# Two cross-attention and feed-forward layers on one core: the first query step of the second attention for four batches at a time, and the output projection started head by head

## The chip, the cores and the metric

The kernel runs on one core of a Trainium2 chip. The metric is the device time of one execution in microseconds (us). Three executions of the kernel before gave 836.81, 837.28 and 837.96 us; the time before is their median, 837.28 us.

## The reference, cut to what matters

The input `x` has B = 8 batches of T = 100 tokens and D = 512 features, and every batch has a context of 361 rows of 128 numbers. Each of two layers adds an attention over the context and a feed-forward part to `x`. The change touches only the second attention and what follows it:

```
q_hk   = layernorm(x) @ Wq.T                      # 16 heads of 128
q_r    = (q_hk @ w_kc_q) @ W_qr                   # 64 numbers per head
k_r    = rope(ctx) @ W_kr                         # per head
attn   = softmax(q_r . k_r)                       # 100 x 361 per head
ctx_c  = attn @ rope(ctx)                         # 128 numbers per head
x     += (ctx_c @ w_kc_kv.T, all heads) @ Wo.T
x     += ffn of the second layer, weights and activations rounded to 8 bits
```

## The kernel before, in words

Nearly all products are made in three parts: an operand is split into a rounded high part (made by ScalarE, ACT) and a low part (made by VectorE, DVE), and `mm3` (lines 149 to 151) runs high x high, high x low and low x high. Each engine has its own program, and semaphores tie them together.

**Preparation.** The query weights are folded into `NFH`/`NFL` (line 1333 and around): eight blocks of 128 columns, each with two heads of 64. `ln_transposes`, `ln_high`, `ln_low` and `normalise` (lines 107 to 131) bring the normalised tokens of a batch into `XHC`/`XLC`. They use two PSUM banks in turn.

**Queries.** `pe_queries` makes the queries of two batches (a pair q = 0..3) in 12 steps. Steps 0 to 3 are the first step: each makes two head blocks, 4 chunks x 3 parts x 2 blocks = 24 products of 200 columns (two batches of 100 tokens), and ACT and DVE (`act_queries` line 949, `dve_queries` line 1791) move 400 columns out into `QRH`/`QRL`. Steps 4 to 11 are the second step: products of 64 rows with `WKH`/`WKL` (line 1363), two heads at a time, moved out into `QH`/`QL` by the same two lines. The first pair's queries come before the attention; those of pair q are made during the second batch of the pair before.

**Attention.** A batch has 1600 rows (16 heads x 100 tokens), that is 13 tiles of 128. Per tile: scores S (mm3 of 362 columns), maximum on DVE (`nmx`, line 1810), exponential on ACT (line 973), normalisation on POOL (line 831), transposes PT on PE (line 1407), high and low part (`pt_hi` line 979, `pt_lo` line 1813), and, per group of tiles, the products PV with the values (384 or 448 columns), which ACT moves out (`ctxo`, line 987). `pair_steps` is a table of ticks: 13 S ticks of the first batch, 13 of the second, then 12 query ticks PR. Everything else is placed behind its due tick; the last five PT of a pair fall on query ticks 0, 2, 4, 6 and 8. All engines walk through this one table: batch 0, then a loop of three passes over (odd batch, even batch), then batch 7 ("last").

**Output.** `pe_fold_p` (line 1384) folds the output weights of the 16 heads; ACT makes `pf_hi` (line 1123) and DVE `pf_lo` (line 1993). The context rows come back from memory in 7 tiles of 128 tokens (`load_ctx`, line 714), are split by `split_ctx` (line 1119) and `low_ctx` (line 1989), and `project(n, ...)` makes 16 heads x 3 products of 512 columns into bank 6, which `add_out` (line 2003) adds to the tokens. Then the last feed-forward part runs, its first products in line 1589; projections 2 to 6 lie between its products in quarters.

SP issues the loads in the order of its program. The folded weights' loads (`load_foldp`), the first context tile, the feed-forward weights `W1Q`, `S1B`, `W2Q`, `S2B` and the later context tiles follow each other there.

Of the kernel before, what the change touches and what calls it, by code (L numbers as in the profile page):

```python
# [96 lines left out]
def build_kernel(nc, x, ctx_t, wq0_t, wkv0_t, wout0_t, ident_d, mask_d, wg_t, w12_d, w3_d, route_d,  # L97
                 ctxn_d, cos_d, sin_d, foldq_d, krt_d, foldp_d,
                 wup_d, wdown_d, wupt_d, wdownt_d, out):
    with ExitStack() as top:  # L100
# [171 lines left out]
        YG_PLACES = [YG_AT + 4 * D * i for i in range(9)] + [2 * FQB + 4 * D * i for i in range(4)] + [W3_AT + 4 * D * i for i in range(3)]  # L272
# [13 lines left out]
        QRH = sc_("qr_hi", [128, NP1, 2 * T], F32R)  # L286
        QRL = sc_("qr_lo", [128, NP1, 2 * T], F32R)
# [18 lines left out]
        FPR_PLACES = [25600, 41984, 47104, 52224, 58368, 65536, 73728]  # L306
# [59 lines left out]
        FPR.append(wraw[:, 0:2 * FP].rearrange("p (h n) -> p h n", h=2))  # L366
# [162 lines left out]
        def _(sp):  # L529
# [155 lines left out]
            for b in range(B):  # L685
# [10 lines left out]
                for g in range(NG):  # L696
# [8 lines left out]
                    elif b == B - 1 and g < 3:  # L705
# [9 lines left out]

            load_foldp(NP1 - 1)
# [4 lines left out]
            sp.dma_start(W2Q[:, :, :], w2_scratch).then_inc(FFNW, 16)  # L721
            sp.dma_start(S2B[:, :], sc_scratch[0:1, 2 * FI:2 * FI + D].broadcast_to((128, D))).then_inc(FFNW, 16)
            for n in range(1, NTT):
                load_ctx(n)
                if n == 2:
# [12 lines left out]
        def _(pool):  # L738
# [48 lines left out]
            pool.wait_ge(E["ups"], NBLK)  # L787
# [12 lines left out]
            def rope(n, j, part):  # L800
# [22 lines left out]
            def pool_steps(kind, n, j):  # L823
                for step in attention_steps(kind):
# [21 lines left out]
            with pool.Fori(0, B // 2 - 1) as p:  # L846
                pool_steps("odd", 2 * p + 1, 1)
# [89 lines left out]
        def queries_part(k, hi):  # L937

            if k < 4:
                o = (QRH if hi else QRL)[:, 2 * k:2 * k + 2, :]  # L940
# [1267 lines left out]
```

## Time and profile before

| | |
|---|---|
| median of three executions | 837.28 us |
| the profiled execution's own time | 830.72 us |
| its span in the trace | 828.9 us |
| granted TensorE clock, mean of the span | 0.932 |
| PE busy | 690.5 us (83%) |
| DVE busy | 510.2 us (62%) |
| ACT busy | 416.0 us (50%) |
| POOL busy | 247.3 us (30%) |
| share of PE in the chain that ended last | 59% |

The profiled execution is one execution with its own time; its span is the part between the first and the last recorded instruction. PE is TensorE's matmuls, PEld its weight loads, which overlap with the matmuls. The granted clock is a share of full speed: 0.5 is the lower level of 1.2 GHz, 1.0 the upper one of 2.4 GHz. The stages are: first attention until 165 us, routing and experts until 354 us, folding and gathering until 394 us, second attention until 645 us, output projection and last feed-forward part until 829 us.

### The profile page before, as it was taken

To read this page: it belongs to the slowest core of one execution; us is meant where nothing else is said; L and a number is where in the kernel's file an instruction comes from. 1 tells how busy PE (TensorE), PEld (TensorE's weight loads), DVE (VectorE), ACT (ScalarE), POOL (GpSimd) and SP (SyncE) were. 2 spreads that over 40 slices of the span, in tenths; PEclk is the share of its full clock that TensorE was granted. 3 is DMA by queue.
4 is the path that set the end of the run, shared out by engine and by line. 5 is a ranking of instruction groups with operands and counts; after the bars stand their busy time and mean duration, and the time that the engine had idled before them with its cause. 6 is when DMAs were issued, how large, how long until landed. Compare 5 with 4: busy or idle time off the path is not lost.

```text
span 828.9 us, 13011 instructions
## 1 busy us (share of the span) xinstructions
PE 690.5 (83%) x4427; PEld 552.5 (67%) x4427; DVE 510.2 (62%) x1038; ACT 416.0 (50%) x777; POOL 247.3 (30%) x278
## 2 busy tenths in 40 slices
PE   0799999654999999992988988988988698799985
PEld 0587777453777777692867877878867375566542
DVE  4876677474666666538476476476475623677674
ACT  3513566363555555321377477476475522455452
POOL 2000742332122222054066166085073001122232
PEclk9987999765999999996799999999999999999997
DMA  8565842598675665698001223123257952111000
GB/s 260 192 209 145 297 147 59 185 390 302 188 228 176 188 184 162 206 297 202 12 1 50 60 50 85 42 60 77 64 172 201 387 191 70 52 52 39 13 14 28
DMA packets 82964, 118.90 MB, mean 143 GB/s; under 512 B 40769, under 2 KB 63037, under 8 KB 79329
## 3 DMA queue, kind: packets, MB, share of 16 engines
q1 hardware_dynamic: 79777, 109.71, 41.6%
q0 software_dynamic: 3136, 8.53, 4.1%
q8 instruction: 30, 0.49, 0.2%
q14 instruction: 21, 0.17, 0.1%
HBM read 97.15 MB, written 27.62 MB: 151 GB/s over the span
## 4 chain that ended last, share of the span: by engine, by line
PE 59%; DVE 15%; ACT 9%; issue 8%; DMA 5%; POOL 1%; ACTq 1%; SPq 0%; DVEq 0%; POOLq 0%
PE PS L149 14%; PE PS L151 12%; PE PS L150 12%; PE PS L1231 4%; PE PS L1407 3%; PE PS L1292 3%; PE PS L1589 2%; DMA raw<-wkv_in 2%; DMA yg<-ys_scratch,slots 2%; DVE nmx L1810 2%; ACT w_hi L884 1%; PE PS L1384 1%; ACT cx_hi L1119 1%; DMA cx_raw<-tile_scratch 1%; ACT wraw L973 1%
## 5 line engine op out<-in xcount | busy, mean ns | idle before, releaser
L831 POOL TENSOR_TENSOR wraw<-wraw,rinv 128x361 f32<-128x361 f32 (+1 forms) x104 | 80.9, 787 | 127.2 <-DVE rinv L1803 126.3
L1646 DVE TENSOR_TENSOR w_lo<-w,w_hi 128x1408 fp32r<-128x1408 f32 x40 | 64.9, 1623 | 39.7 <-ACT w_hi L884 39.7
L973 ACT ACTIVATE wraw<-PS,nmx 128x361 f32<-128x361 f32 (+1 forms) x104 | 58.6, 564 | 30.8 <-DVE nmx L1810 17.8
L1810 DVE TENSOR_REDUCE nmx<-PS 128x1 f32<-128x361 f32 (+1 forms) x104 | 55.1, 531 | 30.3 <-PE PS L151 30.3
L859 POOL TENSOR_TENSOR wraw<-gs,us 128x352 f32<-128x352 f32 (+1 forms) x28 | 26.7, 953 | 139.8 <-ACT gs L1147 112.2
L1813 DVE TENSOR_TENSOR pt_lo<-PS,pt_hi 128x384 fp32r<-128x384 f32 (+1 forms) x104 | 55.7, 535 | 16.3 <-ACT pt_hi L979 15.0
L884 ACT CAST w_hi<-w 128x1408 fp32r x40 | 54.7, 1369 | 18.6 <-DMA w<-w_in 9.4
L784 POOL DMA_INDIRECT xb<-xn_scratch,rows x20 | 31.8, 1589 | 106.6 <-PE PS L1203 103.5
L1407 PE MATMUL PS<-ident,wraw 128*128 128x128 f32 x312 | 52.2, 276 | 11.3 <-DVE pt_lo L1813 5.5
L149 PE MATMUL PS<-w_hi,xt_hi 128*128 128x352 f32 x160 | 56.9, 355 | 5.6 <-DVE xt_lo L1640 5.4
L149 PE MATMUL PS<-pf_hi,cx_hi 128*128 128x512 f32 (+1 forms) x112 | 48.1, 429 | 11.8 <-DVE x_tiles L2003 4.5
L1231 PE MATMUL PS<-w,ht 128*128 128x512 f32 (+1 forms) x120 | 54.9, 593 | 0.7 <-DVE ht L1658 0.7
L979 ACT CAST pt_hi<-PS 128x384 fp32r<-128x384 f32 (+1 forms) x104 | 48.4, 466 | 11.9 <-PE PS L1407 11.8
L1407 PEld LDWEIGHTS PS<-ident,wraw 128*128 128x128 f32 x312 | 38.1, 140 | 23.1 <-issue 10.9
L151 PE MATMUL PS<-w_hi,xt_lo 128*128 128x352 f32 x160 | 52.5, 328 | 0.0
L150 PE MATMUL PS<-w_lo,xt_hi 128*128 128x352 f32 x160 | 52.4, 328 | 0.0
L151 PE MATMUL PS<-pf_hi,cx_lo 128*128 128x512 f32 (+1 forms) x112 | 45.6, 407 | 0.0
L150 PE MATMUL PS<-pf_lo,cx_hi 128*128 128x512 f32 (+1 forms) x112 | 45.5, 406 | 0.0
L149 PE MATMUL PS<-kt_hi,q_hi 128*128 128x362 f32 (+1 forms) x104 | 42.2, 405 | 2.0 <-DVE q_lo L1791 2.0
L149 PE MATMUL PS<-pt_hi,kn_hi 128*128 128x384 f32 (+1 forms) x96 | 36.2, 377 | 9.0 <-ACT ctxo L987 3.8
L115 PE MATMUL PS<-ident,xn 100*128 100x100 f32 x64 | 10.8, 312 | 38.9 <-DVE xn L129 38.1
L149 PEld LDWEIGHTS PS<-w_hi,xt_hi 128*128 128x128 f32 x160 | 30.9, 193 | 18.3 <-DVE xt_lo L1640 18.3
(270 smaller groups left out, 1937.1 us busy)
## 6 DMA issues: line engine op xcount, KB each, us to landing
w<-w_in SPq DMA_DIRECT2D x20, 768.0 KB, 5.5
w<-w_in SPq DMA_DIRECT2D x8, 1408.0 KB, 11.4
fq_raw<-foldq_in SPq DMA_DIRECT2D x6, 1088.0 KB, 7.8
cx_raw<-tile_scratch SPq DMA_DIRECT2D x6, 1024.0 KB, 5.1
ys_scratch<-yb SPq DMA_DIRECT2D x20, 256.0 KB, 5.5
ctx_scratch<-ctxo SPq DMA_DIRECT2D x24, 192.0 KB, 1.9
fp_raw<-foldp_in SPq DMA_DIRECT2D x7, 640.0 KB, 5.0
wraw<-wup_in SPq DMA_DIRECT2D x12, 256.0 KB, 4.3
```

The lines of the kernel that those rows point to most:

```text
L149: pe.matmul(o, lh, rh, start=start, stop=False)
L150: pe.matmul(o, lh, rl, start=False, stop=False)
L151: return pe.matmul(o, ll, rh, start=False, stop=stop)
L831: pool.tensor_tensor(P1[slot][0:rows, 0:NK], P1[slot][0:rows, 0:NK], rinv[0:rows, jj, t:t + 1].broadcast_to((rows, NK)), ALU.mult).then_in ...
L884: act.copy(WH[which][:, :], w12_of(act_whi.e, which)).then_inc(WHS[which], 1)
L973: act.activation(P1[t % 8][r, 0:NK], PS[r, t % 4, 0:NK], ACT.Exp, bias=nmx[r, jj, t:t + 1], accum_out=rsum[r, jj, t:t + 1]).then_inc(C["ex ...
L979: act.copy(pt_place(PTH, t), turned(t)).then_inc(C["pth"], 1)
L1231: last = pe.matmul(PS[:, 4 + i % 2, :], HT[i % 2][0:rows, c * 128:(c + 1) * 128], W3R[i % 2][0:rows, c * D:(c + 1) * D], start=(c == 0), s ...
L1407: last = pe.transpose(PS[:, 4 + t % 3, c * 128:(c + 1) * 128], P1[t % 8][:, c * 128:(c + 1) * 128], ident[:, :])
L1646: dve.tensor_tensor(WL[which][:, :], w12_of(dve_wlo.e, which), WH[which][:, :].bitcast(F32), ALU.subtract) \
L1810: dve.tensor_reduce(nmx[r, jj, t:t + 1], PS[r, t % 4, 0:NK], AX.X, ALU.max, negate=True).then_inc(C["max"], 1)
L1813: dve.tensor_tensor(pt_place(PTL, t), turned(t), pt_place(PTH, t).bitcast(F32), ALU.subtract) \
```

## The change

1. The first query step is done for four batches at once: 8 steps, one head block each, 12 products of 400 columns. It is run for pairs 0 and 2 alone (16 query ticks); pairs 1 and 3 have only the 8 ticks of the second step, which reads its half of the 400 columns. `QRH` and `QRL` are twice as large. Before the attention, four batches are normalised and turned instead of two.
2. The loops of the second attention are written out on all engines.
3. Output: projection 0 no longer waits for all 16 low parts of the folded weights but for one head at a time; projection 1 goes to bank 7 and doesn't wait for `add_out(0)`; projection 2 waits for `add_out(0)` alone. Context tile 0 is split after head 9 instead of head 12, tile 2 before `act_xev(0, 0)`. `W2Q` and `S2B` are loaded behind context tile 1 instead of ahead of it.
4. Places in SBUF move: the gathered expert rows, and folded weights 6, which are now loaded when all transposes of the last batch are done.

```diff
-        def pair_steps(last, vector):
+        def pair_steps(last, vector, asked):
             ticks = [("S", b, t) for b in range(2) for t in range(RT)]
-            ticks += [("PR", 2, k) for k in range(12)] if not last else []
+            ticks += [("PR", 2, k) for k in asked] if not last else []
...
+        FIRST, SECOND = 8, 8
+        def asked_in(q):
+            return range(FIRST + SECOND) if q % 2 == 0 else range(FIRST, FIRST + SECOND)
+        def asked_at(q, k):
+            return 24 * (q // 2) + (k if k < FIRST else k + q % 2 * SECOND)
...
-                if i == NP1 - 1:
+                if i >= NP1 - 2:
                     sp.wait_ge(C["pt"], RT * B)
...
+            load_foldp(NP1 - 2)
             load_foldp(NP1 - 1)
             load_ctx(0)
...
-            sp.dma_start(W2Q[:, :, :], w2_scratch).then_inc(FFNW, 16)
-            sp.dma_start(S2B[:, :], ...).then_inc(FFNW, 16)
             for n in range(1, NTT):
                 load_ctx(n)
+                if n == 1:
+                    sp.dma_start(W2Q[:, :, :], w2_scratch).then_inc(FFNW, 16)
+                    sp.dma_start(S2B[:, :], ...).then_inc(FFNW, 16)
...
-            if k < 4:
-                for m in (2 * k, 2 * k + 1):
-                    for c in range(KC):
...
-                        last = mm3(pe, PS[:, k, m % 2 * 2 * T:(m % 2 + 1) * 2 * T], NFH[:, c, m * 128:(m + 1) * 128],
-                                   NFL[:, c, m * 128:(m + 1) * 128], xh, xl, c == 0, c == KC - 1)
+            if k < FIRST:
+                bank_free(k)
+                x = slice(q // 2 * 4 * T, (q // 2 + 1) * 4 * T)
+                for c in range(KC):
+                    last = mm3(pe, PS[:, k % 4, 0:4 * T], NFH[:, c, k * 128:(k + 1) * 128], NFL[:, c, k * 128:(k + 1) * 128],
+                               XHC[:, c, x], XLC[:, c, x], c == 0, c == KC - 1)
...
-            with pe.Fori(0, B // 2 - 1) as p:
+            for p in range(B // 2 - 1):
                 pe_steps(pe, "odd", 2 * p + 1, 1, p + 1)
                 pe_steps(pe, "even", 2 * p + 2, 0)
...
-                if h == NH0 - 4:
+                if h == NH0 - 7:
                     split_ctx(0, 0)
...
-                    wait(pe, O["res"], n)
+                    wait(pe, O["res"], n if n > 2 else n - 1)
                 for h in heads:
+                    if n == 0:
+                        pe.wait_ge(O["pfl"], h + 1)
...
-            pe.wait_ge(O["pfl"], NH0)
...
+                if n == 0:
+                    pe.wait_ge(O["res"], 2)
...
-            ln_low(dve, 2, 0, XHC, XLC)
-            normalise(dve, 2, 2)
-            ln_low(dve, 2, 1, XHC, XLC)
-            normalise(dve, 2, 3)
+            for b in range(B // 2):
+                ln_low(dve, 2, b, XHC, XLC)
+                normalise(dve, 2, b + 2)
```

The first place is DVE's queue between the last maximum of an odd batch (`nmx` 64x1, not shown) and the first maximum of the next batch, in the query ticks. `qr_lo` is the first step's low part, `q_lo` the second step's, `pt_lo` that of a transposed tile. Before, in every pass:

```order
L1791 TENSOR_TENSOR qr_lo<-PS,qr_hi 128x400
L1813 TENSOR_TENSOR pt_lo<-PS,pt_hi 128x3x128
...
L1791 TENSOR_TENSOR q_lo<-PS,q_hi 128x2x2x100
L1813 TENSOR_TENSOR pt_lo<-PS,pt_hi 128x3x64
...
L1791 TENSOR_TENSOR q_lo<-PS,q_hi 128x2x2x100
L1810 TENSOR_REDUCE nmx<-PS 128x1
```

Now, for the queries of pairs 1 and 3:

```order
L1813 TENSOR_TENSOR q_lo<-PS,q_hi 128x2x2x100
L1835 TENSOR_TENSOR pt_lo<-PS,pt_hi 128x3x128
...
L1813 TENSOR_TENSOR q_lo<-PS,q_hi 128x2x2x100
L1835 TENSOR_TENSOR pt_lo<-PS,pt_hi 128x3x64
L1832 TENSOR_REDUCE nmx<-PS 128x1 x2
```

For pairs 1 and 3 the four `qr_lo` are gone, the five last `pt_lo` lie between the eight `q_lo`, and the 64-column `pt_lo` comes behind the last of them. For pair 2 eight `qr_lo` come first, all but one of the last five `pt_lo` lie between them, and seven `q_lo` follow with nothing between.

The second place is ACT's queue behind the second attention: `pf_hi` are the folded weights' high parts, `cx_hi` the context tiles', `xqt` the turned feed-forward input. Before:

```order
L1123 CAST pf_hi<-PS 128x512 x13
L1119 CAST cx_hi<-cx_raw 128x2048
L1123 CAST pf_hi<-PS 128x512 x3
L1119 CAST cx_hi<-cx_raw 128x2048
...
L1134 ACTIVATE xn_end<-xn_end,mgc,wraw 128x512
L1141 COPY xqt<-PS 128x512
L1119 CAST cx_hi<-cx_raw 128x2048
```

Now:

```order
L1141 CAST pf_hi<-PS 128x512 x10
L1137 CAST cx_hi<-cx_raw 128x2048
L1141 CAST pf_hi<-PS 128x512 x6
L1137 CAST cx_hi<-cx_raw 128x2048
...
L1152 ACTIVATE xn_end<-xn_end,mgc,wraw 128x512
L1137 CAST cx_hi<-cx_raw 128x2048
L1159 COPY xqt<-PS 128x512
```

Tile 0's split moved three heads ahead, and tile 2's ahead of the copy that lets the feed-forward part start. DVE's `cx_lo` of tile 0 moved in the same way, from behind 14 heads to behind 11.

## Rows read from the trace of the kernel before

**Rows 1.** Busy time by stretch, one loop pass: us, then each engine's busy time, clock, DMA
```profile
504.00:563.00 59.00, 53.35 (x378) 47.26 (x378) 35.55 (x93) 36.98 (x103) 28.01 (x37) 1.00 0.27 62
```
**Rows 2.** Timeline of PE, queries of a pair: start us, us, engine, line; 18 products apart
```profile
520.19 0.27 PE L149 MATMUL PS<-xnTc_hi,nf_hi 128*128 x1
...
522.20 0.28 PE L149 MATMUL PS<-xnTc_hi,nf_hi 128*128 x1
```
**Rows 3.** Timeline of PE, first attention, products of 400 columns, 36 apart
```profile
57.77 0.34 PE L149 MATMUL PS<-xnT_hi,hi 128*128 128x400 f32 x1
...
64.36 0.34 PE L149 MATMUL PS<-xnT_hi,hi 128*128 128x400 f32 x1
```
**Rows 4.** Timeline of PE, queries of pair 0, 18 products apart, and batch 0's first score
```profile
398.64 0.41 PE L150 MATMUL PS<-xnTc_lo,nf_hi 128*128 128x200 f32 x1
...
402.48 0.41 PE L150 MATMUL PS<-xnTc_lo,nf_hi 128*128 128x200 f32 x1
...
419.72 0.43 PE L149 MATMUL PS<-kt_hi,q_hi 128*128 128x362 f32 x1 [1.97 <-DVE q_lo L1791]
```
**Rows 5.** Busy time by stretch: query ticks 0 to 3, then 4 to 11, of pair 2
```profile
516.20:529.90 13.70, 13.70 (x115) 13.37 (x114) 3.46 (x7) 3.82 (x8) 0.90 (x2) 1.00 0.24 54
529.90:538.18 8.28, 7.48 (x71) 6.25 (x71) 5.99 (x12) 5.11 (x13) 0.00 (x0) 1.00 0.20 49
```
**Rows 6.** Groups of DVE's instructions, 395 to 646 us: busy us, mean ns, idle before
```profile
L1813 DVE TENSOR_TENSOR pt_lo<-PS,pt_hi 128x384 fp32r<-128x384 f32 (+1 forms) x104 | 55.7, 535 | 16.3 <-ACT pt_hi L979 15.0
...
L1791 DVE TENSOR_TENSOR q_lo<-PS,q_hi 128x400 fp32r<-128x400 f32 x32 | 17.4, 569 | 3.1 <-ACT q_hi L949 3.0
```
**Rows 7.** Timeline of PE's weight loads: first of a pass; first behind the loop
```profile
494.60 0.19 PEld L149 LDWEIGHTS PS<-kt_hi,q_hi 128*128 128x128 f32 x1 [0.26 <-issue]
...
612.19 0.19 PEld L149 LDWEIGHTS PS<-kt_hi,q_hi 128*128 128x128 f32 x1
```
**Rows 8.** Timeline of DVE and PE, batches normalised ahead of the queries
```profile
397.08 0.57 DVE L125 TENSOR_TENSOR xnTc_lo<-PS,xnTc_hi 128x400 fp32r<-128x400 f32 x1
397.56 0.54 DVE L129 TENSOR_SCALAR xn<-X,mv,rstd 100x512 f32<-100x512 f32 x1
...
398.33 0.52 PE L149 MATMUL PS<-xnTc_hi,nf_hi 128*128 128x200 f32 x1
```
**Rows 9.** Timeline from the folded weights to the first feed-forward products, with idle and releaser
```profile
646.46 8.82 PE L1384 MATMUL PS<-fp_raw 128*128 128x512 f32 x20 [1.93 <-DVE pf_lo L1993]
...
657.97 2.28 DVE L1989 TENSOR_TENSOR cx_lo<-cx_raw,cx_hi 128x2048 fp32r<-128x2048 f32 x1
...
661.51 0.50 PE L149 MATMUL PS<-pf_hi,cx_hi 128*128 128x512 f32 x1 [4.51 <-DVE pf_lo L1993]
...
662.66 0.63 PE L150 MATMUL PS<-pf_lo,cx_hi 128*128 128x512 f32 x1
663.09 0.63 PE L151 MATMUL PS<-pf_hi,cx_lo 128*128 128x512 f32 x1
...
675.45 0.47 PE L149 MATMUL PS<-pf_hi,cx_hi 128*128 128x512 f32 x1 [1.15 <-DVE x_tiles L2003]
...
686.45 0.40 PE L1578 MATMUL PS<-identb,xq 128*128 128x128 bf16 x4
...
687.62 1.35 PE L1589 MATMUL PS<-w1q,xqt 128*128 128x352 bf16 x8 [0.77 <-ACT xqt L1141]
...
692.34 0.47 PE L149 MATMUL PS<-pf_hi,cx_hi 128*128 128x512 f32 x1 [3.37 <-DVE x_tiles L2003]
...
696.76 1.37 PE L1589 MATMUL PS<-w1q,xqt 128*128 128x352 bf16 x8
```
**Rows 10.** DMA issues, 600 to 720 us (KB, us to landing), and the split of tile 1
```profile
s_rows<-sc_scratch SPq DMA_DIRECT2D x1, 1408.0 KB, 16.9
w2q<-w_scratch SPq DMA_DIRECT2D x1, 1408.0 KB, 19.4
...
670.47 1.91 ACT L1119 CAST cx_hi<-cx_raw 128x2048 fp32r<-128x2048 f32 x1 [12.16 <-DMA cx_raw<-tile_scratch]
```

More of the change, by code:

```diff
@@ L471, in group_cols, with projected_bank @@
             return ROWS - 384 * g if g == NG - 1 else 384
+        def projected_bank(n):
+            return 7 if n == 1 else 6
         def tile_rows(t):
@@ L821, in rope_low, with pool_steps @@
                 pool.tensor_tensor(KNL[j][:, :, :], kvr[:, :, :], KNH[j][:, :, :].bitcast(F32), ALU.subtract).then_inc(C["knl"], 1)
-            def pool_steps(kind, n, j):
-                for step in attention_steps(kind):
+            def pool_steps(kind, n, j, q=None):
+                for step in attention_steps(kind, q):
                     what, dn, t = step
@@ L966, in act_steps @@
         def act_steps(act, kind, n, j, q=None):
-            for what, dn, t in attention_steps(kind):
+            for what, dn, t in attention_steps(kind, q):
                 m, jj = (n, j) if dn == 0 else (n + dn, 1 - j)
@@ L1102, in _ @@
             lnc_act(act)
-            ln_high(act, 2, 0, XHC)
-            ln_high(act, 2, 1, XHC)
+            for b in range(B // 2):
+                ln_high(act, 2, b, XHC)
             act_keys(act, 0, 0)
-            for k in range(12):
-                if k % 2 == 0:
-                    ln_high(act, 2, 2 + k // 2, XHC)
+            for k in asked_in(0):
+                if k < FIRST and k % 2 == 0:
+                    ln_high(act, 2, B // 2 + k // 2, XHC)
                 act_queries(act, 0, k)
             act_steps(act, "even", 0, 0)
-            with act.Fori(0, B // 2 - 1) as p:
+            for p in range(B // 2 - 1):
                 act_steps(act, "odd", 2 * p + 1, 1, p + 1)
@@ L1362, in pe_queries @@
                             r = slice(half * R1, (half + 1) * R1)
-                            last = pe.matmul(PS[:, (k + half) % 4, (m - k + 4) * 2 * T:(m - k + 5) * 2 * T], w[r, m, :], x[r, m, :],
+                            last = pe.matmul(PS[:, (k + half) % 4, (m - heads[0]) * 2 * T:(m - heads[0] + 1) * 2 * T], w[r, m, :], x[r, m, mine],
                                              start=(x is QRH and w is WKH), stop=(w is WKL), tile_position=(half * R1, 0))
@@ L1387, in pe_steps @@
         def pe_steps(pe, kind, n, j, q=None):
-            for what, dn, t in attention_steps(kind):
+            for what, dn, t in attention_steps(kind, q):
                 m, jj = (n, j) if dn == 0 else (n + dn, 1 - j)
@@ L1803, in invert @@
                 dve.reciprocal(rinv[r, jj, t:t + 1], rsum[r, jj, t:t + 1]).then_inc(C["inv"], 1)
-            for what, dn, t in attention_steps(kind, vector=True):
+            for what, dn, t in attention_steps(kind, q, vector=True):
                 m, jj = (n, j) if dn == 0 else (n + dn, 1 - j)
@@ L1981, in _ @@
             dve_steps(dve, "even", 0, 0)
-            with dve.Fori(0, B // 2 - 1) as p:
+            for p in range(B // 2 - 1):
                 dve_steps(dve, "odd", 2 * p + 1, 1, p + 1)
```

95 lines of the change are left out of this document (49 added, 46 removed).

## The prediction

> **What bounds the kernel now.** I read the time by stretch first, then PE's timeline in the stretches that the change touches, then the idle times there, DVE's groups, and last the DMA issues.
>
> In one pass of the second attention's loop (59 us for two batches) PE is busy 53.35 us, DVE 35.6, ACT 37.0, at the full clock [rows 1]. So PE is the bound. In the query ticks this is stronger: in ticks 0 to 3, the first query step, PE is busy for all of 13.70 us and DVE for 3.5; in ticks 4 to 11, the second step, PE is busy 7.48 of 8.28 us and DVE 5.99 [rows 5]. The first is pure PE time, the second is close to a chain PE, ACT, DVE. Behind the attention, PE waits 4.51 us before projection 0, 1.15 us before projection 1 and 3.37 us before projection 2 [rows 9]. These waits are on DVE, on the path that ends last.
>
> **The price of a product.** 18 products of 200 columns start 2.01 us apart: 0.112 us each [rows 2]. 36 products of 400 columns, also with a new weight load each, take 6.59 us: 0.183 us [rows 3]. Two of the first cost 0.223 us, one of the second 0.183. Per four batches, 192 products become 96. The first step of pairs 0 and 1 (or 2 and 3) costs 192 x 0.112 = 21.4 us before and 96 x 0.183 = 17.6 now: 3.8 less, twice, 7.6 in all if the clock is full and nothing else comes to bind.
>
> The Trainium skill speaks against this term: "TensorE: Matmul & The Clock Gate", Back-to-back issue gap, gives the isolated gap at the upper clock as columns / 2.4 + 2.5 ns. As an estimate by that page, two products of 200 columns take 171.7 ns and one of 400 takes 169.2, so the term would be 0.5 us, not 7.6. Rows 2 disagree with it for the small product (112 ns against 85.8); the page itself says that weight loads count in a real stream.
>
> **Part by part, in the second attention.**
>
> Pair 0 gets longer. (a) Two more batches are turned first. On DVE each costs 0.57 us for the low part and 0.54 for normalising [rows 8]: 2 x 1.11, with the last turn's latency about +2.5 us; queries start near 400.8 instead of 398.33. (b) The clock is at its lower level here: 0.213 us per product [rows 4], until about 402.9, just behind these rows. Before, 22 products at 0.213 and 74 at 0.112 made 13.0 us. At the lower level a product of 512 columns takes 0.43 us [rows 9], so one of 400 takes 0.43 x 400 / 512 = 0.34. If the clock rises at the same moment, 6 products at 0.34 and 90 at 0.183 make 18.5 us: +5.5. (c) All four remaining turns now lie inside the first step, two more than before, some 0.4 us each: +0.8. (d) The second step loses them: its eight `q_lo` at 0.569 [rows 6] and a lead of about 1 us make 5.5 us, where before it took 419.72 - 398.33 - 13.0 - 0.8 (two turns) = 7.6 [rows 4, 8], with four low parts and three normalisings between: -2.1. Sum **+6.7 us**. Bounds: +6.0 if the turns overlap better, +8.5 if the clock rises one or two microseconds later (each costs 0.45).
>
> Pairs 1 and 3 lose 96 x 0.112 = 10.7 us each. Their cover goes too: the last five transposed tiles, two of which lay under ticks 0 to 3, now share eight ticks with the eight `q_lo`. DVE then has 8 x 0.569 + 5 x 0.535 = 7.2 us [rows 6] in about 11 us, and its last `pt_lo` stands behind the last `q_lo`, with PV and the next scores behind it. The second step already shows 0.8 us of idle PE in 8.28 [rows 5]; I double the stalls' density over the longer piece: +1.7 us. So **-9.0 us each**, between -10.7 (no stall) and -6 (ACT and DVE bind all through, 1.1 us a tick more than PE needs).
>
> Pair 2 grows by 96 x (0.183 - 0.112) = +6.8 us. Its second step has no transposed tiles left, save one, and becomes a chain bound by DVE of 5.5 us; the PE work moved out of it now lies in the PE-bound first half. Idle PE grows from 0.8 to perhaps 1.6: **+7.6 us**, between 6.5 and 8.5.
>
> Writing out the loops: a pass begins with a PE wait of 0.26 us for issue that the batch behind the loop doesn't have [rows 7]. Three passes, less what the wait hides: **-0.5 us**, bounds -0.8 and 0.
>
> By the Trainium skill, "Runtime: NRT & Kernel Launch", Instruction fetch mechanics, a taken branch to code outside the two resident blocks costs a fetch by DMA. Rows 7 show 0.26 us at the jump, so I take this value; a fetch at each jump would add gains that no row here shows.
>
> Attention in all: 6.7 - 18.0 + 7.6 - 0.5 = **-4.2 us**.
>
> **Part by part, behind the attention.**
>
> Projection 0 now starts where the first head's low part and `cx_lo` are there. PE makes ten heads in 8.82 us, 0.88 each [rows 9]. ACT's split (1.91 us as for tile 1 [rows 10]) comes three heads earlier, but the context tile is then just landing; DVE's 2.28 us for `cx_lo` then stand ahead of `pf_lo` of head 11, for which PE's head 15 waits. The fold is delayed by about 3 us and ends near 660.2 instead of 661.51 - 4.51 = 657.0; projection 0 follows at once, near 660.2 instead of 661.51: **-1.3 us**, between -2.5 and +0.5.
>
> PE's longest idle time falls from 4.51 us to about 2. Before, the clock fell behind it: products of 512 columns took 0.43 us [rows 9]. Projection 0 took 13.94 - 1.15 = 12.8 us, projection 1 the same 48 products in 11.0. The idle time of 1.93 us ahead of the fold was not followed by such a fall, so I take the full clock: **-1.7 us**, or 0.
>
> Projection 1 waited 1.15 us for `add_out(0)`. Bank 7 removes that. Its other need, context tile 1, landed only at 670.47 [rows 10], because W2Q and S2B were ahead of it in the queue; W2Q landed 2.5 us (plus 0.5 between the issues) behind S1B [rows 10]. Without both, tile 1 lands some 4 us earlier, near 666.5, its high and low parts (1.9 and 2.3 us) are done at 670.7, and projection 0 ends at 671.2. So the wait goes whole: **-1.2 us**, or +1 if the tile lands no earlier.
>
> Between projection 1's end at 686.45 and projection 2's start at 692.34 lie 5.9 us: turn, 0.77 us of waiting, 1.35 of gate and up, and 3.37 of waiting for split, `cx_lo` and `add_out(1)` of the old order [rows 9]. Tile 2 is now split ahead of `xqt`, and `add_out(1)` is not waited for. 2.5 us remain: **-3.4 us**, or -1 if tile 2, which waits for W2Q and S2B now, lands late. The quarter of projection 2 then took 696.76 - 692.34 = 4.4 us for 12 products, against 12 x 0.229 = 2.75 at the full clock: **-1.6 us**, or 0 if the clock falls here all the same.
>
> The rest of the feed-forward part hangs on this start through PE, DVE and the tile loads, and I let it move as a whole. Sum -9.2 us. The loads of folded weights 6 come 3 us later, behind the last transposes; head 12 needs them 7 us after that, so nothing. The memset of POOL that waits for the last expert products ends before the stores it waits for anyway: nothing.
>
> **Sum.** -4.2 - 9.2 = -13.4 us. Against the profiled execution's own 830.72 us that is 817.3. The median, 837.28, is 6.6 us above that one; I subtract the same amount there: **823.9 us**.
>
> **Rivals.**
>
> *A, half the tail.* The clock falls behind the shorter idle times too and the rest of the feed-forward part gives back part of the start, since it waits for DVE in places. The loss is 1.7 + 1.6 + about 1.5: 828.7. For it: PE still rests about 2 us between single heads before projection 0. Against it: 1.93 us did no harm.
>
> *B, the short ticks bind.* In pairs 1 and 3 ACT and DVE set the pace: -6 instead of -9, twice: 829.9. For it: DVE's 7.2 us and ACT's equal load in 11 us, in chains. Against it: the second step runs with PE 90% busy now.
>
> *C, columns are all that counts.* The 400-column product costs twice the 200-column one, 0.223 us: the 7.6 us are gone, 831.5. Rows 3 are the same kind of product at 0.183, so little speaks for it.
>
> *D, slower, by the written-out code.* Two further copies of the loop's body are fetched. A pass has 378 products and 378 weight loads on PE [rows 1], so some 1500 more instructions in blocks that could stall PE at each fetch. It decides from 13.4 us on over, say, six blocks, 2.2 us each; at 5 us each it would be 853. Against it: batch 7 stands outside the loop, and its first score is issued without even the 0.26 us [rows 7].
>
> *E, no change.* The clock stays low through pair 0's whole first step: 90 x (0.34 - 0.183) = +14 us, 838. The chip would have to keep it low under a busy PE, while before it rose after 8 us.
>
> **How the numbers follow.** A measurement of this kernel can tell about 0.2%, 1.7 us, from no change. Chances: forecast 0.58 (820 to 827), A 0.17, B 0.10, C 0.06, E 0.03, D 0.04, and 0.02 for more than the forecast. Forecast, A, B, and C lie over 1.7 us below: with the last, 0.93 faster. E is 0.03 same. D is 0.04 slower. The range 819.5 to 831 takes in the forecast's unknowns (all lower bounds -9, upper +5), A and B.
>
> **What would show it.** In the profile after: first-step products 0.18 us apart, 96 per four batches; pair 0's first score near 426.5; from the first score of batch 2 to that of batch 4, and of 4 to 6, 66.5 and 50 us instead of 59 twice (pair 2's queries lie in the first, pair 3's in the second, pair 1's ahead of both); projection 0 at the full clock, projection 1 with no wait, projection 2 within 3 us of projection 1's end. Wrong it would be if PE stands idle over 3 us in the queries of pairs 1 and 3, if a stretch of written-out code shows waits for issue, or if the last part of the kernel, from projection 2 on, takes longer than now.

## The result and the profile after

The changed kernel took 826.0 us (median of four executions, 824.61 to 829.34), the kernel before 837.62 beside it on the same chip (836.81 to 838.48): a ratio of 0.9863, 95% interval 0.982 to 0.9906, or 11.6 us less. The forecast was 823.9, range 819.5 to 831.

The traces don't show 11.6 us. The profiled execution of the changed kernel took 826.05 us, just its median; the one of before had been 830.72, 6 us under the fastest execution timed beside it. Against that profiled execution the prediction had 817.3 us, and 826.05 is 8.7 more. So the two are compared stretch by stretch. The changed kernel's page (first line, part 1, and the first line of part 4):

```profile
span 824.0 us, 12030 instructions
...
PE 688.8 (84%) x4235; PEld 550.3 (67%) x4235; DVE 511.2 (62%) x1038; ACT 416.0 (50%) x777; POOL 249.4 (30%) x278
...
PE 55%; DVE 14%; issue 13%; ACT 8%; DMA 4%; POOL 2%; ACTq 1%; SPq 1%; another core or an unknown queue 0%; DVEq 0%; POOLq 0%
```

PE is as busy as before (690.5 us there): fewer products, but more of them at the low clock. Its timeline in the queries of pair 0 (start us, us, engine, line; in brackets the idle time before and what ended it), beside [rows 4]:

```profile
402.87 0.68 PE L149 MATMUL PS<-xnTc_hi,nf_hi 128*128 128x400 f32 x1
403.36 0.54 PE L150 MATMUL PS<-xnTc_lo,nf_hi 128*128 128x400 f32 x1
...
407.69 0.38 PE L151 MATMUL PS<-xnTc_hi,nf_lo 128*128 128x400 f32 x1
407.91 0.35 PE L149 MATMUL PS<-xnTc_hi,nf_hi 128*128 128x400 f32 x1
...
423.92 0.36 PE L1381 MATMUL PS<-qr_hi,wkr_hi 64*128 64x200 f32 x2
...
430.71 0.67 PE L149 MATMUL PS<-kt_hi,q_hi 128*128 128x362 f32 x1 [1.61 <-DVE q_lo L1813]
```

Its busy times over the first two parts of that (us, then each engine's busy time, clock, DMA):

```profile
402.87:407.69 4.82, 4.82 (x17) 4.77 (x15) 1.25 (x3) 0.92 (x2) 0.81 (x1) 0.50 0.00 0
408.00:423.90 15.90, 15.90 (x94) 15.52 (x92) 5.71 (x11) 4.14 (x9) 0.00 (x0) 1.00 0.00 1
```

The first 15 products run at the low clock, 0.333 us apart; the rest are 0.183 apart. Behind the attention, beside [rows 9] and [rows 10] (timeline of PE, ACT and DVE):

```profile
655.07 1.90 ACT L1137 CAST cx_hi<-cx_raw 128x2048 fp32r<-128x2048 f32 x1 [1.20 <-DMA cx_raw<-tile_scratch]
...
658.10 2.28 DVE L2010 TENSOR_TENSOR cx_lo<-cx_raw,cx_hi 128x2048 fp32r<-128x2048 f32 x1
658.33 1.10 PE L1402 MATMUL PS<-wraw 128*128 128x512 f32 x2 [1.64 <-DVE pf_lo L2014]
...
661.04 2.07 PE L1402 MATMUL PS<-wraw 128*128 128x512 f32 x2 [1.61 <-DVE pf_lo L2014]
662.12 1.42 PE L149 MATMUL PS<-pf_hi,cx_hi 128*128 128x512 f32 x1
663.33 0.63 PE L150 MATMUL PS<-pf_lo,cx_hi 128*128 128x512 f32 x1
663.76 0.63 PE L151 MATMUL PS<-pf_hi,cx_lo 128*128 128x512 f32 x1
...
669.09 1.91 ACT L1137 CAST cx_hi<-cx_raw 128x2048 fp32r<-128x2048 f32 x1 [5.35 <-DMA cx_raw<-tile_scratch]
...
686.73 0.40 PE L1598 MATMUL PS<-identb,xq 128*128 128x128 bf16 x4
687.89 1.35 PE L1609 MATMUL PS<-w1q,xqt 128*128 128x352 bf16 x8 [0.77 <-ACT xqt L1159]
688.96 0.52 PE L149 MATMUL PS<-pf_hi,cx_hi 128*128 128x512 f32 x1
691.85 1.37 PE L1609 MATMUL PS<-w1q,xqt 128*128 128x352 bf16 x8
```

Projection 2 starts 2.2 us behind the turn of xq instead of 5.9, without a wait, and its first quarter is over after 2.9 us instead of 4.4. But PE waits twice in the fold (1.64 and 1.61 us), and projection 0 still starts at the low clock (0.43 us a product).

The same stretches in all the traces, worked out from starts in PE's timeline, in us. "q0", "q1" ... are the queries of pair 0, 1 ...: q0 from the first turn to the first score of batch 0, the others from the last score of the batch ahead to the first of the next; "to last" from the first turn to the last score; "P0" from there to projection 0; "P0-xq" on to the first turn of xq; "xq-P2" on to projection 2; "quarter" on to its second quarter. From there to the end it is 129.5 to 132.3 us in all of them. A score is the product of keys and queries (`kt_hi,q_hi`), a turn the transpose of a batch's normalised tokens (line 115).

| kernel | first turn at | q0 | q1 | q2 | q3 | to last | P0 | P0-xq | xq-P2 | quarter |
|---|---|---|---|---|---|---|---|---|---|---|
| before | 394.6 | 25.08 | 24.11 | 24.09 | 24.11 | 236.2 | 30.69 | 24.94 | 5.89 | 5.50 |
| before again (e4) | 390.4 | 24.37 | 24.10 | 24.09 | 24.10 | 235.3 | 30.69 | 25.45 | 5.89 | 5.32 |
| loops only (e1) | 393.7 | 25.25 | 23.69 | 23.69 | 23.72 | 233.6 | 30.69 | 25.40 | 5.88 | 5.44 |
| attention only (e2) | 392.6 | 33.30 | 14.37 | 32.14 | 14.35 | 232.1 | 32.41 | 25.38 | 5.89 | 5.49 |
| tail only (e3) | 391.3 | 24.63 | 24.11 | 24.10 | 24.11 | 235.8 | 29.98 | 24.33 | 2.23 | 3.98 |
| **after** | 396.6 | 34.10 | 15.36 | 32.12 | 15.81 | 235.6 | 29.91 | 24.61 | 2.23 | 3.98 |
| after again (e5) | 401.3 | 34.12 | 15.87 | 32.10 | 14.36 | 234.2 | 30.03 | 23.27 | 2.24 | 3.96 |
| loops and tail (e6) | 401.4 | 25.24 | 23.69 | 23.71 | 23.69 | 233.5 | 30.17 | 24.28 | 2.23 | 3.98 |
| spacing (e7) | 400.7 | 34.02 | 12.43 | 32.13 | 12.43 | 228.3 | 29.57 | 23.59 | 2.23 | 3.97 |
| halves (e8) | 402.2 | 37.23 | 15.85 | 36.10 | 14.36 | 241.8 | 29.96 | 24.41 | 2.24 | 3.94 |
| pieces (e9) | 406.3 | 34.10 | 12.45 | 32.12 | 12.43 | 228.9 | 25.66 | 27.91 | 2.24 | 3.97 |
| pieces, busy PE (e10) | 403.6 | 32.04 | 12.43 | 32.13 | 12.43 | 226.3 | 25.71 | 28.25 | 2.23 | 3.98 |
| old W2Q (e11) | 402.4 | 24.57 | 24.10 | 24.10 | 24.11 | 235.7 | 30.16 | 25.37 | 2.23 | 3.98 |
| old projection 0 (e12) | 409.6 | 25.62 | 24.10 | 24.14 | 24.10 | 236.5 | 30.73 | 24.26 | 2.24 | 3.97 |

Between before and after, the change gives 0.6 us up to the last score and 6.3 behind it. The four queries together take 97.4 us in both traces: what pairs 1 and 3 gain, pairs 0 and 2 lose. The first turn comes 2.0 us later, in a part that the change hardly touches; this start lies at 390 to 394 on the chip of e1 to e4, at 401 to 402 on the one of e5 to e8 and at 402 to 410 on the one of e9 to e12, so it says nothing of the change. What goes with it is the clock: ahead of the first turn its records add up to 80.4 us at the lower level in before and 84.4 in after, 71 to 75 in e1 to e4, 84 to 90 in e5 to e8 and 82 to 100 in e9 to e12. P0-xq also follows the clock: in after, e3 and e5, the same code there, it is 24.61, 24.33 and 23.27 us with 5.1, 4.5 and 2.3 us at the lower level in it.

### The profile page after: what moved, and what is told of

The parts are those of the page before. It is cut to its first block, busy times and chain, and to the rows that moved or that the text cites. A ratio compares the mean times of both kernels' runs of the same rounds, so it can differ in the third digit from the quotient of the medians.

```text
span 824.0 us, 12030 instructions
## 1 busy us (share of the span) xinstructions
PE 688.8 (84%) x4235; PEld 550.3 (67%) x4235; DVE 511.2 (62%) x1038; ACT 416.0 (50%) x777; POOL 249.4 (30%) x278
## 4 chain that ended last, share of the span: by engine, by line
PE 55%; DVE 14%; issue 13%; ACT 8%; DMA 4%; POOL 2%; ACTq 1%; SPq 1%; another core or an unknown queue 0%; DVEq 0%; POOLq 0%
PE PS L149 12%; PE PS L151 11%; PE PS L150 10%; PE PS L1249 3%; PE PS L1425 3%; PE PS L1310 3%; PE PS L1609 2%; ACT w_hi L902 2%; DMA raw<-wkv_in 2%; DVE wscale L1867 1%; PE PS L1340 1%; POOL wraw L849 1%; PE PS L1351 1%; PE PS L1629 1%; DVE X L1972 1%
## 5 line engine op out<-in xcount | busy, mean ns | idle before, releaser
L800 POOL DMA_INDIRECT xb<-xn_scratch,rows x20 | 35.1, 1756 | 103.7 <-PE PS L1221 100.6
L1425 PE MATMUL PS<-ident,wraw 128*128 128x128 f32 x312 | 51.7, 275 | 11.6 <-DVE pt_lo L1835 5.5
```

What stands on the lines that cost most here:

```text
L1425: last = pe.transpose(PS[:, 4 + t % 3, c * 128:(c + 1) * 128], P1[t % 8][:, c * 128:(c + 1) * 128], ident[:, :])
```

## The experiments

Each group of four ran on one chip, with its own executions of before; the ratio is to those.

| run | median us | before beside it | ratio (95% interval) |
|---|---|---|---|
| e1 loops only | 827.72 | 831.29 | 0.9963 (0.9946 to 0.9981) |
| e2 attention only | 829.28 | 831.29 | 0.9993 (0.9971 to 1.0015) |
| e3 tail only | 822.36 | 831.29 | 0.9903 (0.9875 to 0.9931) |
| e4 before again | 830.18 | 831.29 | 0.9994 (0.9973 to 1.0014) |
| e5 after again | 825.99 | 838.6 | 0.985 (0.9802 to 0.9898) |
| e6 loops and tail | 826.82 | 838.6 | 0.9867 (0.9819 to 0.9916) |
| e7 spacing | 821.54 | 838.6 | 0.9808 (0.9755 to 0.986) |
| e8 halves | 837.9 | 838.6 | 0.9993 (0.996 to 1.0025) |
| e9 pieces | 827.22 | 841.46 | 0.9825 (0.9781 to 0.9868) |
| e10 pieces, busy PE | 825.67 | 841.46 | 0.9838 (0.9784 to 0.9892) |
| e11 old W2Q | 833.45 | 841.46 | 0.9906 (0.9867 to 0.9945) |
| e12 old projection 0 | 833.15 | 841.46 | 0.9883 (0.9825 to 0.994) |

### The change in parts: loops, attention, tail

**e1**, the kernel before with the loops written out:

```diff
-            with pe.Fori(0, B // 2 - 1) as p:
+            for p in range(B // 2 - 1):
```

and the same on ACT, DVE and POOL.

> The kernel before with nothing changed but that the three passes of the second attention's loop are written out on PE, ACT, DVE and POOL. Theory 1 (the prediction's): the jump costs 0.26 us a pass, so 0.5 us less than before (0.06%), which this measurement can't tell from nothing. Theory 2: the medians lie 11.6 us apart while the two traces account for only about 7 us in the stretches the change touches (0.6 in the attention, 6.3 behind it); the rest is a cost of the loop's jumps that varies from execution to execution and that the one profiled execution of before (830.72 us against a median of 837) happened not to show. Then this kernel is 4 to 6 us faster than before. Theory 3: written-out code costs fetches: slower by 1 us or more.

3.1 us less by the ratio (1.6 to 4.5), 1.7 to 2.6 in the traces, up to the last score. The queries of pairs 1, 2 and 3 are 0.4 us shorter each, and the stretches of scores between them 0.1 to 0.5, by small steps. Two of the places in PE's timeline of before:

```profile
477.40 0.44 PE L149 MATMUL PS<-pt_hi,kn_hi 128*128 128x448 f32 x1 [0.29 <-DVE pt_lo L1813]
...
488.07 0.41 PE L149 MATMUL PS<-pt_hi,kn_hi 128*128 128x384 f32 x1 [0.31 <-DVE pt_lo L1813]
```

and the same products in e1:

```profile
475.90 0.47 PE L149 MATMUL PS<-pt_hi,kn_hi 128*128 128x448 f32 x1
...
486.06 0.44 PE L149 MATMUL PS<-pt_hi,kn_hi 128*128 128x384 f32 x1
```

In the loop PE stood 0.3 us waiting for DVE's low part, written out it doesn't. The two pages count 13,011 and 12,412 instructions: in the loop the counts that waits compare with are worked out in registers. That this is what makes the handovers slow is my reading; no run separates it. My theory 2, a cost that varies, asked for 4 to 6 us. The queries of pairs 1 to 3 are 24.1 us in both traces of before, so what the traces show is a steady cost. Whether there is a varying one beside it stays open: the interval of the ratio reaches 4.5 us, and the executions of before here spread over 8.0 us, those of e1 over 3.9.

One of my signs of being wrong was a written-out stretch that waits for issue. By the label it came: e1's trace has waits of 0.37 and 0.72 us "for issue" on PE in its attention, and after's has one of 1.79 us before batch 4's first score. They show no fetch. Before has 0.62 us at the place of the first 0.72 of them, put down to ACT's `ctxo`, and at 616.4, in batch 7 outside the loop, 0.71 us for issue; the 1.79 us end when DVE's last `q_lo` does (it starts at 546.88 and takes 1.53 us for three). And e1 is faster with them:

```profile
548.52 0.40 PE L149 MATMUL PS<-kt_hi,q_hi 128*128 128x362 f32 x1 [1.79 <-issue]
```

**e2**, the change without its tail (the fold's old heads for splitting tile 0, one bank, the old order of loads and of tile 2's split; the new places and loads of the folded weights stay).

> The change without its tail: the context tile is split at the old heads, projection 0 waits for the whole fold, one bank for the projections, W2Q and S2B ahead of tile 1, old place of tile 2's split. Theory 1 (prediction): 4.2 us less than before, with 0.5 of it from the loops. Theory 2 (the traces): from the first turn of the queries to the start of the fold of heads the trace of after is only 0.6 us shorter (251.3 against 251.8), so this kernel gives 0.6 us, and 5 to 6 if the loops alone give 4 to 6. Theory 3: four-batch products give nothing and written-out code nothing: the same as before.

Not told from before (0.6 us less by the ratio, between 2.4 less and 1.2 more), and 1.6 us slower than the loops alone by the medians. Its trace is 3.2 to 4.1 us shorter up to the last score, yet most of its executions aren't: they reach from 825.2 to 834.0. A likely reason, which no trace of e2's longer executions shows, is in the next section: q1 and q3 are 14.4 us here and up to 15.9 in the traces of after. In this trace the clock also fell in the fold (P0 32.41 instead of 30.69).

**e3**, the tail alone.

> The kernel before with its attention, loops and two-batch queries kept, and only what the change does behind the attention: context tile 0 split three heads earlier, projection 0 by heads, bank 7 for projection 1, tile 1 loaded ahead of W2Q and S2B, tile 2 split ahead of act_xev, and the places and loads of the folded weights that the earlier split needs. Theory 1 (prediction): 9.2 us less than before. Theory 2 (the traces): from the start of the fold to the end the trace of after is 6.3 us shorter, so 6.3 us less. Rival A of the prediction: half, 4.6 us less.

8.1 us less by the ratio (5.7 to 10.4), 8.9 by the medians; the trace gives 0.7 + 1.1 + 3.7 + 1.3 = 6.8 against e4. The tail is most of the change's gain; with the loops' 3.1 it makes 11.2 of the 11.6 us.

**e4**, before again.

> The kernel before, unchanged, profiled and timed a second time. If its profiled execution was an unusually short one, this profile comes out near the median of 837 us and shows where the 6.6 us lie: by theory 2 of the loops, as idle time behind the jumps at the start of passes (batches 1, 3, 5); otherwise in the stage of the experts or the gather ahead of 394 us, where the profile of after has 1.3 and 0.5 us of waiting for issue on PE that the one of before hasn't. If it comes out at 830 again, profiled executions of this kernel are shorter than timed ones, and the two of before and after can't be compared by their totals.

Its profiled execution is the fastest of the twelve (826.03, median 830.18). The first turn comes 4.3 us earlier than in the first trace, all else agrees within 1 us, and most stretches to 0.1. So the total of one profiled execution is uncertain by some 4 us, while its stretches can be compared.

### Four batches at a time: what it gives, and where it goes

**e5**, after again.

> The changed kernel, unchanged, timed and profiled a second time, beside the others of this call. Its two halves gave -2.0 us (attention only, interval from -2.4 to +1.2) and -8.9 us (tail only): if they add up it is about 0.987 of before. The profile decides a point of its own: in the trace of after, the clock stood at its lower level for some 3 us behind the 1.73 us of idle PE that end the queries of pairs 1 and 3 (from the last score of batch 1 to the first of batch 2 15.36 us, pair 3's 15.81), and in the trace of the attention alone, the same code there, it did not (14.37, 14.35). If this fall is an accident of the execution, this profile shows either length; if it belongs to the kernel as a whole, it shows 15.4 and 15.8 again.

0.985, as the first time. The fall of the clock is not fixed by the code: within this one execution it is there in q1 (15.87), not in q3 (14.36). In the first trace of after (timeline of PE, from the last score of batch 1 to the first of batch 2):

```profile
466.29 0.41 PE L149 MATMUL PS<-kt_hi,q_hi 128*64 128x362 f32 x1
...
478.71 0.47 PE L149 MATMUL PS<-pt_hi,kn_hi 128*128 128x448 f32 x1 [1.73 <-DVE pt_lo L1835]
479.02 0.37 PE L150 MATMUL PS<-pt_lo,kn_hi 128*128 128x448 f32 x1
...
479.78 0.58 PE L150 MATMUL PS<-pt_lo,kn_hi 128*128 128x448 f32 x1
...
481.65 0.51 PE L149 MATMUL PS<-kt_hi,q_hi 128*128 128x362 f32 x1
```

and in e2, the same code:

```profile
461.00 0.41 PE L149 MATMUL PS<-kt_hi,q_hi 128*64 128x362 f32 x1
...
473.44 0.47 PE L149 MATMUL PS<-pt_hi,kn_hi 128*128 128x448 f32 x1 [1.73 <-DVE pt_lo L1826]
473.74 0.36 PE L150 MATMUL PS<-pt_lo,kn_hi 128*128 128x448 f32 x1
473.95 0.36 PE L151 MATMUL PS<-pt_hi,kn_lo 128*128 128x448 f32 x1
...
475.37 0.33 PE L149 MATMUL PS<-kt_hi,q_hi 128*128 128x362 f32 x1
```

The same 1.73 us of idle PE, and once the products behind it are 0.37 us apart, once 0.20. The busy times of after say the clock:

```profile
478.00:480.00 2.00, 1.29 (x5) 1.20 (x6) 0.66 (x2) 0.00 (x0) 0.00 (x0) 0.86 0.39 91
480.00:482.00 2.00, 2.00 (x7) 1.80 (x7) 0.00 (x0) 0.11 (x1) 0.00 (x0) 0.50 0.00 0
```

**e6**, loops written out and the whole tail, queries as before.

> The loops written out and the whole tail, but the queries as before, two batches at a time. Loops alone gave -3.1 us, the tail alone -8.9: together -12.0, a ratio of 0.9855. Theory 1 (the traces of the attention without clock falls): four batches at a time are worth another 1.5 us (from the first turn to the last score 232.1 us against 233.6), so this kernel is 1.5 us slower than after. Theory 2: they are worth nothing or less, since the 400-column products start at the low clock in pair 0 and the short pairs end with idle PE, behind which the clock falls in most executions: this kernel is as fast as after or up to 2.5 us faster (loops alone -3.1 against attention only -0.6).

826.82 against 825.99 for after: not told apart. To the last score 233.5 us against 234.2 and 235.6 for after, 232.1 for e2. Beside it, e2 was 1.6 us slower than e1 by the medians. So the part of the title with four batches and 400 columns gives nothing here that times or traces can tell, where the forecast had 3.7 us.

**e7**, the tighter spacing:

```diff
+            apart = 1 if len(asked) == SECOND and not last else 2
...
-                    at = at + LAG if at + LAG < 2 * RT else 2 * RT + 2 * (at + LAG - 2 * RT)
+                    at = at + LAG if at + LAG < 2 * RT else 2 * RT + apart * (at + LAG - 2 * RT)
```

> The changed kernel; in the two short pairs (eight ticks of queries) the last five transposed tiles stand one tick apart instead of two, as they had been placed for twelve ticks. Theory 1: the 1.73 us of idle PE ahead of the last PV (it waits for the last low part on DVE, behind the last q_lo) goes in both pairs, with the clock fall that follows it in some executions (1.0 and 1.45 us in the trace of after): 3 to 5.5 us less than after again, and from the last score to the first 13 us instead of 14.4 to 15.8. Theory 2: ACT and DVE bind the short ticks (eight q_lo and five pt_lo make 7.2 us of DVE, and ACT has as much): the idle time only moves ahead into the ticks, and the gain is below 1 us.

821.54 us, 4.4 less than after again beside it by the medians, 3.5 by the ratios, and 5.9 in the trace up to the last score. PE's timeline at the end of the queries of pair 1:

```profile
479.38 0.27 PE L1382 MATMUL PS<-qr_hi,wkr_lo 64*128 64x200 f32 x2
479.66 0.47 PE L149 MATMUL PS<-pt_hi,kn_hi 128*128 128x448 f32 x1
...
481.60 0.32 PE L149 MATMUL PS<-kt_hi,q_hi 128*128 128x362 f32 x1
```

No wait before the last PV, no fall behind it; q1 and q3 are 12.43 us. ACT and DVE didn't bind the short ticks; theory 2 fell. **This version beats both kernels**, 17 us under before there, and e6 by 5.3 us (5.2 in the trace up to the last score). So four batches at a time do give some 5 us over two, once the transposed tiles are spaced for the eight ticks. Two batches at a time with the tighter spacing weren't run; PE is idle for only 0.8 us in each of the queries of e6's pairs 1 to 3, which bounds what it could gain there.

**e8**, halves:

```diff
-                for c in range(KC):
+                for u, c in [(u, c) for u in range(2) for c in range(KC)]:
```

with the 200 columns of half u in each product.

> The changed kernel, but each product of 400 columns in the first query step is issued as two of 200, in the same ticks. Theory 1 (products at the trace's prices, 0.112 and 0.183 us): pair 2's first step takes 192 x 0.112 = 21.5 instead of 17.6 us, +3.9, and pair 0's some 22 x 0.213 + 170 x 0.112 = 23.7 instead of 14.5 x 0.333 + 81.5 x 0.183 = 19.7, +4.0: about 7.9 us slower than after again, products 0.11 us apart. Theory 2 (the gap by the formula columns/2.4 + 2.5 ns): +0.5 us. Theory 3: something else, ACT or DVE, bounds the first step: no change.

q2 is 4.0 us longer, as forecast, q0 3.1. Its products in pair 2 (18 apart) take the 0.112 us of [rows 2]:

```profile
527.93 0.28 PE L149 MATMUL PS<-xnTc_hi,nf_hi 128*128 128x200 f32 x1
...
529.94 0.36 PE L149 MATMUL PS<-pt_hi,kn_hi 128*128 128x384 f32 x1
```

(the second is the next piece of work, 18 products later). So the price of width is shown: 0.112 for 200 columns, 0.183 for 400, and the 0.5 us of theory 2 doesn't hold for this stream. The formula in the Trainium skill's "TensorE: Matmul & The Clock Gate", Back-to-back issue gap, is for a single isolated product, and the page says itself that it leaves out the weight load at small widths; the trace agrees with that, 112 ns against 86. By the medians the halves cost 11.9 us, by the trace 7.5 up to the last score and 1.1 in P0-xq; the rest I can't place.

### The tail in parts

**e11** undoes the order of the loads (W2Q and S2B ahead of tile 1 again), **e12** the early split of tile 0 and the start by heads; both on e3's kernel.

> The tail alone (queries and loops as before) with one part undone: W2Q and S2B are loaded ahead of tile 1 again. Theory 1: tile 1 lands some 3 to 4 us later, at 12 us behind its issue instead of 8, and projection 1, which with the tail alone started without a wait, waits 1 to 2 us for it: 1 to 2 us slower than the tail alone (ratio 0.9903). Theory 2: the two loads were not what kept tile 1: no change.

> The tail alone with another part undone: context tile 0 is split at the old heads (behind head 12 on ACT, 13 on DVE) and projection 0 waits for the whole fold. Theory 1: the two waits of 1.6 us in the fold go, one of 4.5 us before projection 0 comes back, so the early split was worth only the 0.7 us that the traces show (last score to projection 0 29.98 us against 30.69). Theory 2 (the prediction's): 1.3 us and, with the clock, 3.

The wait before projection 1 in e11, which e3 hasn't, and the one before projection 0 in e12:

```profile
682.58 0.50 PE L149 MATMUL PS<-pf_hi,cx_hi 128*128 128x512 f32 x1 [0.86 <-DVE cx_lo L1998]
```

```profile
676.83 0.79 PE L149 MATMUL PS<-pf_hi,cx_hi 128*128 128x512 f32 x1 [4.51 <-DVE pf_lo L2002]
```

The order of loads is worth 1.0 us (P0-xq 25.37 against 24.33), theory 1. The early split is worth 0.75 (P0 30.73 against 29.98) and nothing with the clock, theory 1 again. The ratios can't resolve either. What is left of the tail, 3.7 + 1.3, is tile 2's split ahead of act_xev and projection 2 that no longer waits for add_out(1); it wasn't undone by itself. Nor was bank 7: e11, which has it, needs 25.37 us for P0-xq and e4, which hasn't, 25.45, so without the earlier tile 1 it showed no gain.

**e9**, on e7: tile 0 in four pieces.

```diff
-                if h == NH0 - 7:
-                    split_ctx(0, 0)
+                if NH0 - 6 <= h < NH0 - 2:
+                    c = h - (NH0 - 6)
...
+                    act.copy(CXH[0][:, c * 512:(c + 1) * 512], CXR[:, c * 512:(c + 1) * 512]).then_inc(O["cxh"], 1)
```

> The kernel with the tighter spacing, and context tile 0 split in four pieces of four heads: ACT's high parts behind pf_hi of heads 10 to 13, DVE's low parts behind pf_lo of heads 11 to 14, projection 0 waiting for each piece. Theory 1: in all traces with the new tail PE waits 1.6 to 1.9 us before heads 14 and 1.61 us before head 15, since ACT waits for the tile and then splits all of it, and DVE's 2.28 us of cx_lo stand ahead of pf_lo; behind that the clock is low for 5 us of projection 0. With pieces, PE makes the fold without a wait above 1 us, projection 0 starts about 3 us earlier against the last score (26.5 instead of 29.6 to 30.2 us), and the clock stays up (projection 0 some 1.5 us shorter); projection 1 then waits up to 1.5 us for tile 1. Together 3 to 4 us less than the spacing kernel (ratio 0.9808 there). Theory 2: tile 0 lands too late for any of this, or tile 1 becomes what projection 1 waits for: below 1 us.

Projection 0 starts 3.9 us earlier and at the full clock, and all of it is lost before xq (27.91 against 23.59):

```profile
671.84 1.90 ACT L1138 CAST cx_hi<-cx_raw 128x2048 fp32r<-128x2048 f32 x1 [9.00 <-DMA cx_raw<-tile_scratch]
...
673.77 2.29 DVE L2017 TENSOR_TENSOR cx_lo<-cx_raw,cx_hi 128x2048 fp32r<-128x2048 f32 x1 [8.91 <-ACT cx_hi L1138]
...
676.12 0.50 PE L149 MATMUL PS<-pf_hi,cx_hi 128*128 128x512 f32 x1 [3.79 <-DVE cx_lo L2017]
...
678.08 0.63 PE L149 MATMUL PS<-pf_hi,cx_hi 128*128 128x512 f32 x1
```

The raw tile has one buffer. Tile 1 is asked for only when the last piece of tile 0 is split, lands 7.6 us later, and is split whole: projection 1 waits 3.79 us, and behind that the clock falls. What binds here is the way of tile 1. Theory 2's second half; I had put that wait at 1.5 us at most.

**e10**, on e9: 64 products of the identity on PE, whose results nobody reads, while DVE sums up the expert outputs.

> As the one with pieces, and PE has extra work whose results nobody reads: eight turns of the identity (128 columns, fp32) for each batch that DVE sums up while PE otherwise sits idle for 12 to 14 us ahead of the first turn. Theory 1 (the clock is low in pair 0's first step because PE was idle ahead of it): now the first query products run at 0.183 us apart from the start or within a microsecond or two, in place of some 14 at 0.333: 1.5 to 2.5 us less from first query product to first score (25.5 instead of 27.8), and the turns ahead of it are a little shorter. Theory 2: gaps of 1 us between the little groups are enough to keep the clock low: no change, or up to 0.5 us more.

PE is busy and at the full clock from 392, and the clock still falls at the first query product, behind three short gaps at the turns (timeline of PE, then busy times):

```profile
402.68 1.06 PE L1567 MATMUL PS<-ident 128*128 128x128 f32 x8
...
405.73 0.56 PE L115 MATMUL PS<-ident,xn 100*128 100x100 f32 x4 [1.30 <-DVE xn L129]
406.67 0.56 PE L115 MATMUL PS<-ident,xn 100*128 100x100 f32 x4 [0.37 <-DVE xn L129]
...
408.42 0.56 PE L115 MATMUL PS<-ident,xn 100*128 100x100 f32 x4 [0.86 <-DVE xnTc_lo L125]
408.77 0.55 PE L149 MATMUL PS<-xnTc_hi,nf_hi 128*128 128x400 f32 x1
```

```profile
392.00:403.00 11.00, 11.00 (x101) 11.00 (x100) 6.91 (x19) 0.21 (x1) 0.00 (x0) 1.00 0.27 74
...
406.00:408.70 2.70, 1.46 (x14) 1.03 (x13) 2.46 (x6) 1.76 (x4) 0.09 (x1) 1.00 0.00 0
408.80:412.00 3.20, 3.20 (x13) 3.18 (x11) 1.50 (x4) 0.49 (x1) 0.89 (x1) 0.52 0.00 0
```

q0 is 2.1 us shorter than in e9: 1.1 by turns at the full clock, 1.0 by eleven low products instead of fifteen. The times don't tell the two apart: the medians are 825.67 and 827.22, the ratios 0.9838 and 0.9825. Neither theory held: the long idle time wasn't the only cause.

## Why the prediction was right, and where it wasn't

The time was right to 2 us, but not by its steps: by the two traces both large terms were too favourable, the attention by 3.6 us and the tail by 2.9. The 13.4 us of the sum are 6.9 between the traces; the medians gave 11.6.

- **The price of a product**: right, and now measured by e8.
- **Pair 0**, forecast +6.7: +9.0 (34.10 against 25.08), outside the bound of +8.5.
  - (a) Two more turns: 6.26 against 3.69, +2.6, as forecast.
  - (b) failed, in the assumption that the clock rises at the same moment. It rose at 403.0 in before and at 407.8 in after, 4.8 us later, where the queries start 4.5 us later. So 15 products were low instead of 6. In the thirteen traces without e10's extra work the rise lies 3.2 to 5.8 us behind the first query product. First step with turns 21.05 against 13.8, +7.3 instead of +6.3.
  - (d) -0.8 instead of -2.1. My 5.5 us for the second step, worked out from eight `q_lo` and a lead of 1 us, were too few: it takes 6.79 here and 6.47 in the traces where the clock stays full to its end (e2, e7, e8). PE waits some 0.4 us at each pair of its ticks for a `qr_lo` or `q_lo`, and 1.61 at its end.
- **Pairs 1 and 3**, -9.0 each: -8.75 and -8.30, and -9.75 where the clock doesn't fall. The loops' 0.4 us are in these. The stall that I named, PV behind the last `pt_lo`, was there at 1.73 us. What I left out is what the clock makes of it, another 1.0 to 1.5.
- **Pair 2**, +7.6: +8.0, near the forecast, but PE is idle for 2.8 us in it, not 1.6.
- **Loops**, -0.5: -3.1 by the ratio, 1.7 to 2.6 in the traces, outside my bound of -0.8. I had looked at the jump alone [rows 7]; the cost lay spread over the waits of the pass.
- So the attention, forecast -4.2, gave -0.6 us between the traces of before and after, and -1.1 to -4.1 in e5 and e2, by which trace of before one takes.
- **Tail**, -9.2: -6.3 in the trace; in e3 -6.8 in the trace and -8.1 by the ratio.
  - Projection 0's start: -0.8 (forecast -1.3). Its full clock, -1.7, didn't come: PE's longest idle time was cut from 4.51 us to twice 1.6, and the fall still followed, with 5.1 us at the lower level up to the turn of xq against 3.4 before.
  - Projection 1's wait is gone as forecast, but P0-xq is only 0.3 us shorter here (1.1 in e3), since the clock takes the rest back.
  - Turn of xq to projection 2 -3.7 (forecast -3.4), its first quarter -1.5 (forecast -1.6). The rest did move as a whole: 131.1 us in both traces.
- **Rivals.** E and D didn't come, C is refuted by e8; B had -6 for pairs 1 and 3, and both gained over 8. A, half the tail, came half: its clock part was true of projection 0.
- **Signs.** 0.183 us a product and 96 of them, as named; from the first score of batch 2 to that of batch 4, and of 4 to 6, 66.87 and 50.18 us (named: 66.5 and 50). Projection 0 at the full clock was the sign that failed.
- **Range.** The bounds of its parts don't add up to the -9 and +5 that I gave: they make -6.7 and +18.9 us. The range was a choice, not a sum.

Stretch by stretch the two traces give 6.9 us, the medians 11.6 (interval 7.9 to 15.1). Loops and tail by their own ratios make 11.2, by their traces about 9. So 2 to 5 us of the gain lie in no stretch that I compared, and to that extent the forecast was lucky. Where they are stays open. One likely place is the clock of the profiled execution of before: its mean was 0.932. On e5's chip, where the medians of both kernels are nearly the same as here, before's seventeen executions run from 834.17 us at 0.932 to 845.2 at 0.921, and after's six lie at 0.920 to 0.927. For the executions of before that were timed beside after the clock isn't known.

## What to carry to other kernels

Where a change takes cover away, read what the clock does behind the new idle time: 1.7 us of waiting cost 1.0 to 1.5 more in some executions. An idea and its spacing belong together: four batches at a time gave nothing that could be told until one line spaced the elementwise work for the new number of ticks, and then some 5 us. An early start gains nothing while the next thing that it needs (here tile 1, in a single buffer) comes no earlier. And split a change: here the loops and the tail carried it, and the queries of four batches nothing.

## What was not expected of the hardware

The clock's fall behind the same 1.7 us of idle PE came in three of the six short queries in the traces of e2, after and after again, and in one of the two in e8's. Behind pair 2's queries, whose last wait is 1.79 us, it came in e2, e7 and e8 (from 548.9 us in e7) and not in after, e5, e9 and e10. In e10 gaps of 1.30, 0.37 and 0.86 us, with turns between them and 11 us of unbroken work ahead, were followed by 3.2 us at 0.52.

The same kernel before took 831.3, 838.6 and 841.5 us on three chips, with median granted clocks of 0.934, 0.927 and 0.924. There is no trace of it on the last two; over all traces the first turn's start differs by 19 us, and the stretches of the same code behind it by 3.5 us at most (first turn to last score, 232.1 us in e2 and 235.6 in after).
